# Graph attention on one Trainium2 core: the dots of a chunk as one product and one sum

## The chip, the cores and the metric

The kernel runs on one core of a Trainium2 chip (trn2). The metric is the device time of one execution in microseconds, as the median of several executions.

## The reference

One graph attention layer over 12500 nodes with 64 features and 212500 edges sorted by target node, followed by a residual sum and a layer norm:

```python
h_trans = features @ Watt_w.T + Watt_b
h_src, h_dst = h_trans[src], h_trans[dst]
e_raw = jnp.sum(h_dst * jnp.tanh(h_src + e_r), axis=-1, keepdims=True)
e_ij = leaky_relu(e_raw / out_dim ** 0.5)
exp_e = jnp.exp(e_ij - segment_max(e_ij, dst)[dst])
alpha = exp_e / (segment_sum(exp_e, dst)[dst] + 1e-09)
h_neigh = segment_sum(features[src] * alpha, dst)
h_out = leaky_relu((features + h_neigh) @ W1_w.T + W1_b + (features * h_neigh) @ W2_w.T + W2_b)
x = layernorm(x + h_out)
```

The change is in `e_raw`: for each edge, the product of two vectors of 64 values and its sum.

## The kernel before

The edges are cut into 111 blocks of 1920. A block is 15 tiles of 128 edges: partition p holds 15 consecutive edges of the list, so every tile is a column of 64 values a partition. The 15 tiles form four chunks (4, 4, 4 and 3 tiles); chunks 0 and 1 are piece 0, chunks 2 and 3 piece 1. The last block has 11 tiles in chunks of 4, 4, 2 and 1. The edges of a block hit at most 128 consecutive nodes, its window.

Every engine has its own written order of work, one `step` a block, and a step works on several blocks at once: `b`, the one before it (`prev`), the two before that (`before`, `third`) and the next ones (`nxt`, `ahead`, `far`). The steps of four blocks are the body of a loop on the four engines that compute; the first and last blocks stand outside it. What a block goes through:

- GpSimd (POOL) gathers the source rows of its 15 tiles from a table in HBM, one indirect DMA a tile (`gather`, L628), into one of four buffers `got`. The gathers of a piece wait until VectorE has read that piece of the block four before (`scale_rows`, L1290, wait at L626). ScalarE builds `hotT`, the one-hot matrices of the targets (`offsets` L724, `mark_nodes` L735).
- TensorE (PE) expands the window's rows `hw` to one row an edge (`expand`, L949): 15 fp32 products, two passes each, into four PSUM banks `ps_hd[c]`, one a chunk. It starts on a block once `lay_back` (L975) of the block before is issued, which waits for VectorE's `scan_row` (L1257, L1259).
- VectorE adds the gathered row to the edge's attributes (`add`, L1221), ScalarE takes the tanh in place (`tanh`, L750), and VectorE makes the dots (`dot`, L1232): one multiply-and-sum instruction a tile, with the product written back to `edge` and the sum to one column of `raw`. In the trace each is a CUSTOM_DVE_ANT_0 and a DVE_READ_ACCUMULATOR2_ANT.
- `finish_scores` (L1244 to L1250) and `scan_row` find the largest score of each target. In the next step `exponents` (L1266 to L1276), ScalarE's `probabilities`, `scale_rows`, and the split of the scaled rows into three bf16 parts (`left_part` L1297, `low_part` L1303 on VectorE, `high_part` L785 and `mid_part` L790 on ScalarE) feed the sums on TensorE (`sum_edges`, L994). Then come the dense layer and the norm.

VectorE's order in a step is: add of chunk 0, exponents of `prev`, `place(nxt)` (two copies, L1196 and L1198, then `dst_rel`, L1199, which waits on a semaphore for the second copy), the four `build_hot` (L1210), both `scale_rows`, the node work of two older blocks, `set_gaps`, dot 0, add 1, both `left_part`, dot 1, add 2, both `low_part` (the second waits for ScalarE's second `mid_part`), add 3, dot 2, dot 3, `finish_scores`, `scan_row`, and the norm of `third`. Nothing else sets the order.

Of the kernel before, what the change touches and what calls it, by code (L numbers as in the profile page):

```python
# [22 lines left out]
ALU = mybir.AluOpType  # L23
ACT = mybir.ActivationFunctionType
AX = mybir.AxisListType
# [6 lines left out]
CHUNK = 4  # L32
# [21 lines left out]
def gnn_layer(nc, x, src, dst, edge_attr, w1, b1, w2, b2, watt, batt, out):  # L54
    N, D = x.shape
# [29 lines left out]
    SCALE = D ** -0.5  # L85
# [7 lines left out]
    with ExitStack() as ctx:  # L93
        def sb(name, shape, dt=F32):
            return ctx.enter_context(nc.sbuf_tensor(name, shape, dt))

        def bank(name, dt=F32):
            return ctx.enter_context(nc.psum_tensor(name, [P, 512 * 4 // mybir.dt.size(dt)], dt))

        def sem(name):  # L100
            return ctx.enter_context(nc.semaphore(name))

        def by_chunk(name):

            return [sem(f"{name}_{c}") for c in range(NC)]
# [52 lines left out]
        edge = [sb(f"edge{k}", [P, TILES, D]) for k in range(2)]  # L158
        got = [sb(f"got{k}", [P, TILES, 2 * D + 1]) for k in range(BUFS)]

        hw = [sb(f"hw{k}", [P, D]) for k in range(2)]
# [3 lines left out]
        hotT = [sb(f"hotT{k}", [P, TILES, P]) for k in range(2)]  # L165
        raw = [sb(f"raw{k}", [P, TILES]) for k in range(2)]
# [74 lines left out]
        ps_hd = [bank(f"ps_hd{k}") for k in range(CHUNK)]  # L241
# [66 lines left out]
        hd_ready = by_chunk("hd_ready")  # L308
        added = by_chunk("added")
        tanh_done = by_chunk("tanh_done")  # L310
        scored = by_chunk("scored")
        here_set = sem("here_set")
        ids_set = sem("ids_set")
# [78 lines left out]
        def chunks(b):  # L392
            return FINAL_CHUNKS if final(b) else CHUNKS
# [8 lines left out]
        def follows(b, n):  # L402

            return not b.known or b.n >= n

        def cols(b, c):
            return chunks(b)[c][0], chunks(b)[c][-1] + 1
# [5 lines left out]

            return 16 * (b.fours * len(CHUNKS[c]) + len(chunks(b)[c]))

        def expanded(g, c):

            k = g % CHUNK
            return ps_hd[c][:, k * D:(k + 1) * D]

        def node_rows(t, b, a, z):
# [453 lines left out]
        def _(pe):  # L875
# [64 lines left out]
            def expand(b, c):  # L940

                pe.wait_ge(hotT_built[c // 2], b.n + 1)
                if c == 0:
                    pe.wait_ge(h_in[b.two], (b.twos + 1) * 16)
                if follows(b, 1):

                    pe.wait_ge(scored[c], b.n)
                for g in range(*cols(b, c)):
                    last = pe.matmul(expanded(g, c), hotT[b.two][:, g, :], hw[b.two][:, :], start=True, stop=True)  # L949
                last.then_inc(hd_ready[c], 1)  # L950

            def lay_rows(b):
# [65 lines left out]
            def step(third, before, prev, b, nxt, ahead, far):  # L1018
                if exists(third):
                    dense(third)  # L1020
                if exists(b):
                    for c in range(NC):
                        expand(b, c)
                if exists(before):
                    transpose_sum_prod(before)
                if exists(prev) and carried(prev):
                    take_carry(before)
                if exists(prev):
                    sum_edges(prev, 0)
                    sum_edges(prev, 1)  # L1030
                if exists(b):
                    lay_rows(b)
                    lay_back(before, b)
# [39 lines left out]
        def _(dve):  # L1073
# [150 lines left out]
            def dot(b, c):  # L1224

                a, z = cols(b, c)

                dve.wait_ge(consts, 5)
                dve.wait_ge(tanh_done[c], b.n + 1)
                dve.wait_ge(hd_ready[c], b.n + 1)  # L1230
                for g in range(a, z):
                    last = dve.tensor_tensor_reduce(  # L1232
                        out=edge[b.two][:, g, :], in0=edge[b.two][:, g, :],
                        in1=expanded(g, c), scale=SCALE, scalar=0.0,
                        op0=ALU.mult, op1=ALU.add, accum_out=raw[b.two][:, g:g + 1])
                last.then_inc(scored[c], 1)

            def gap_of(b):
                return gap_final if final(b) else gap
# [133 lines left out]
            def step(third, before, prev, b, nxt, ahead, far):  # L1373
# [18 lines left out]
                if exists(b):  # L1392
                    set_gaps(b)
                    dot(b, 0)
                    add(b, 1)
# [3 lines left out]
                if exists(b):  # L1399
                    dot(b, 1)  # L1400
                    add(b, 2)
# [4 lines left out]
                if exists(b):  # L1406
                    add(b, 3)
                    dot(b, 2)
                    dot(b, 3)
                    finish_scores(b)  # L1410
                    scan_row(b)
# [127 lines left out]
```

## Time and profile before

| | |
|---|---|
| median of 3 executions | 2827.87 us (2823.59 to 2828.71) |
| the profiled execution | 2813.21 us |
| its span | 2811.4 us |
| instructions | 32328 |
| PE, share of the span | 49% |
| VectorE (DVE) | 59% |
| ScalarE (ACT) | 57% |
| GpSimd (POOL) | 59% |
| DMA | 296.07 MB, mean 105 GB/s |

The span is the time from the first to the last instruction of one profiled execution. The granted clock of TensorE is 0.5 of full speed in all but the first of 40 slices of the span. The busy shares hardly vary over the span. No engine is busy for more than three fifths of it, so the busy time by itself does not say what the kernel waits for; the timeline of one block does. A line of the timeline gives start and length in microseconds, the engine, the line of the code, the operation, what it writes and reads, how many instructions are merged in it, and in square brackets the idle time before it with what ended it.

### The profile page before, as it was taken

Reading aid. Unit: us, or ns where it says so; the run is one execution under the profiler, and the core shown is the slowest. Engines: PE = TensorE matmul, PEld = TensorE weight load, DVE = VectorE, ACT = ScalarE, POOL = GpSimd, SP = SyncE. Lnnn points to the kernel's source line nnn. Section 1 sums busy time; section 2 is a strip of 40 time slices with the busy share of each in tenths; the row PEclk is TensorE's granted clock in tenths of the full one; section 3 lists DMA queues with packets and bytes.
Section 4 is the critical chain, followed back from the end, with each engine's and each line's share of the span. In section 5 each row is a group of like instructions: output and inputs, shape, how many; then the busy total and the mean of one; then the engine's idle time right before and its main releaser. Section 6 shows DMA issues by size and latency. Waiting matters only on the chain. (4 is left out here: it accounts for less than half of the span.)

```text
span 2811.4 us, 32328 instructions
## 1 busy us (share of the span) xinstructions
PE 1365.9 (49%) x6440; PEld 1096.9 (39%) x6440; DVE 1652.8 (59%) x7936; ACT 1602.6 (57%) x2794; POOL 1655.3 (59%) x1670
## 2 busy tenths in 40 slices
PE   4344444455444444554445444554544555444455
PEld 4333343344333433443334334443433444333344
DVE  2256666655665656565666555655666556566567
ACT  2345555565555555565655556655555565656565
POOL 4466666666665666566666656666566666666660
PEclk7555555555555555555555555555555555555555
DMA  4333333333333333333333333333333333333331
GB/s 162 113 94 101 108 109 108 108 107 97 109 101 107 108 108 108 108 95 105 105 108 109 108 108 100 116 100 100 104 108 109 108 102 102 110 100 108 108 111 31
DMA packets 169270, 296.07 MB, mean 105 GB/s; under 512 B 111730, under 2 KB 111942, under 8 KB 169107
## 3 DMA queue, kind: packets, MB, share of 16 engines
q1 hardware_dynamic: 114689, 185.75, 19.9%
q0 software_dynamic: 53152, 107.98, 15.5%
q14 instruction: 154, 1.26, 0.1%
q10 hardware_dynamic: 1266, 0.93, 0.1%
q8 instruction: 9, 0.15, 0.0%
HBM read 284.43 MB, written 10.07 MB: 105 GB/s over the span
## 5 line engine op out<-in xcount | busy, mean ns | idle before, releaser
L628 POOL DMA_INDIRECT got<-table,src_i x1631 | 1625.7, 997 | 1074.5 <-DVE spare L1290 515.4
L949 PE MATMUL ps_hd<-hw,hotT 128*128 128x64 f32 x3322 | 731.9, 421 | 7.3 <-ACT hotT L735 7.3
L949 PEld LDWEIGHTS ps_hd<-hw,hotT 128*128 128x128 f32 x3322 | 721.9, 333 | 7.5 <-ACT hotT L735 7.5
L994 PE MATMUL ps_acc<-parts,hot 128*128 128x195 bf16 x1661 | 328.3, 364 | 637.9 <-DVE parts L1303 567.2
L750 ACT ACTIVATE edge<-edge 128x256 f32<-128x256 f32 (+1 forms) x444 | 176.6, 398 | 613.8 <-issue 499.8
L994 PEld LDWEIGHTS ps_acc<-parts,hot 128*128 128x128 bf16 x1661 | 208.8, 136 | 744.9 <-issue 619.8
L724 ACT ACTIVATE off<-dst_all,node 128x1024 bf16<-128x1024 int32 x222 | 424.7, 1913 | 121.3 <-remote 73.6
L1303 DVE TENSOR_TENSOR parts<-spare,parts 128x520 bf16<-128x520 f32 x222 | 147.1, 663 | 235.1 <-ACT parts L790 211.8
L1232 DVE CUSTOM_DVE_ANT_0 edge<-edge,ps_hd 128x64 f32<-128x64 f32 x1661 | 265.8, 217 | 18.8 <-remote 7.1
L1005 PE MATMUL ps_misc<-ident,sum_prod 128*128 128x128 f32 x111 | 52.4, 472 | 431.7 <-DVE sum_prod L1319 431.7
L735 ACT ACTIVATE hotT<-off,ones 128x1024 f32<-128x1024 bf16 x222 | 242.6, 1093 | 7.2
L1199 DVE TENSOR_SCALAR dst_rel<-dst_i,base 128x30 bf16<-128x30 int32 (+1 forms) x111 | 27.1, 244 | 365.3 <-remote 262.5
L1221 DVE TENSOR_TENSOR edge<-edge,got 128x256 f32<-128x256 f32 (+1 forms) x444 | 178.8, 403 | 76.3 <-issue 76.3
L1005 PEld LDWEIGHTS ps_misc<-ident,sum_prod 128*128 128x128 f32 x111 | 20.9, 188 | 451.5 <-DVE sum_prod L1319 451.5
L1210 DVE TENSOR_TENSOR hot<-ps_row,dst_rel 128x512 bf16<-128x512 bf16 (+1 forms) x444 | 149.8, 400 | 41.3 <-DVE dst_rel L1199 29.7
L785 ACT ACTIVATE parts<-spare 128x520 bf16<-128x520 f32 x222 | 133.4, 604 | 66.8 <-DVE spare L1290 64.5
L774 ACT ACTIVATE prob<-arg 128x15 f32<-128x15 f32 (+1 forms) x111 | 23.9, 215 | 252.2 <-remote 145.8
L1257 DVE TENSOR_TENSOR_SCAN ps_row<-row_gap,row_max,ps_row 1x256 f32<-1x256 f32 x109 | 81.0, 743 | 134.3 <-remote 52.7
L790 ACT ACTIVATE parts<-spare 128x520 bf16<-128x520 f32 x222 | 134.9, 608 | 24.2 <-DVE spare L1297 20.2
L975 PE MATMUL ps_misc<-ident,row_max 1*128 1x1 f32 x222 | 40.6, 250 | 217.7 <-issue 193.8
L798 ACT ACT_TABLE_LOAD x109 | 139.8, 1283 | 2.0
L975 PEld LDWEIGHTS ps_misc<-ident,row_max 1*128 1x128 f32 x222 | 34.5, 202 | 270.0 <-issue 270.0
(137 smaller groups left out, 1974.1 us busy)
## 6 DMA issues: line engine op xcount, KB each, us to landing
dst_all<-in_dst SPq DMA_DIRECT2D x109, 960.5 KB
edge<-in_edge_attr SPq DMA_DIRECT2D x110, 480.0 KB
got<-table,src_i POOLq DMA_INDIRECT x1631
table<-hx SPq DMA_DIRECT2D x12, 512.0 KB
hw<-table SPq DMA_DIRECT2D x111, 32.0 KB
xw<-in_x SPq DMA_DIRECT2D x111, 32.0 KB
out<-y_out SPq DMA_DIRECT2D x111, 32.0 KB
x_piece<-in_x SPq DMA_DIRECT2D x3, 768.0 KB, 4.4
```

The lines of the kernel that those rows point to most:

```text
L628: pool.indirect_dma_start(got[b.four][:, g, 0:2 * D], None, table, bass.IndirectOffsetOnAxis(ap=src_i[b.four][:, g:g + 1], axis=0))\
L724: act.activation(off[p][:, 0:z - a, :], ids[:, a:z, :], ACT.Abs, bias=node[b.two][:, 0:1])\
L735: act.activation(hotT[b.two][:, a:z, :], off[p][:, 0:z - a, :], ACT.Relu, bias=ones[:, 0:1], scale=-1.0)\
L750: act.activation(edge[b.two][:, a:z, :], edge[b.two][:, a:z, :], ACT.Tanh).then_inc(tanh_done[c], 1)
L790: act.activation(parts[:, a:z, 1, :], rest[:, a:z, :], ACT.Copy).then_inc(rest_mid[p], 1)
L798: act.activation(std1[:, :], mean_var[:, 1:2], ACT.Sqrt, bias=eps_col[:, 0:1]).then_inc(std_set, 1)
L949: last = pe.matmul(expanded(g, c), hotT[b.two][:, g, :], hw[b.two][:, :], start=True, stop=True)
L994: last = pe.matmul(a_parts, hot[b.four][:, g, :], parts[:, g, :, :].rearrange("p a d -> p (a d)"), start=(g == 0), stop=(g == tiles(b) - 1))
L1210: dve.tensor_tensor(hot[b.four][:, a:z, :].rearrange("p g (n a) -> p g n a", a=2), row_iota.rearrange("p (z n a) -> p z n a", z=1, a=2).to ...
L1221: dve.tensor_tensor(edge[b.two][:, a:z, :], edge[b.two][:, a:z, :], got[b.four][:, a:z, 0:D], ALU.add).then_inc(added[c], 1)
L1232: last = dve.tensor_tensor_reduce(out=edge[b.two][:, g, :], in0=edge[b.two][:, g, :], in1=expanded(g, c), scale=SCALE, scalar=0.0, op0=ALU ...
L1303: dve.tensor_tensor(parts[:, a:z, 2, :], rest[:, a:z, :], parts[:, a:z, 1, :], ALU.subtract)\
```

## The change

The dots of a chunk become two instructions. The first multiplies all tiles of the chunk by the expanded rows of the chunk's PSUM bank and by the scale, in place in `edge`. The second sums `edge` along its 64 columns and writes the chunk's columns of `raw`. VectorE waits for the first through a new semaphore a chunk, `multiplied`, before it issues the second. A tile's place in the bank now counts from the first tile of its chunk, which is the same place as before but in the last block's last chunk.

```diff
--- before.py
+++ after.py
@@ -308,6 +308,7 @@
         hd_ready = by_chunk("hd_ready")
         added = by_chunk("added")
         tanh_done = by_chunk("tanh_done")
+        multiplied = by_chunk("multiplied")
         scored = by_chunk("scored")
         here_set = sem("here_set")
         ids_set = sem("ids_set")
@@ -413,9 +414,9 @@
 
             return 16 * (b.fours * len(CHUNKS[c]) + len(chunks(b)[c]))
 
-        def expanded(g, c):
-
-            k = g % CHUNK
+        def expanded(g, b, c):
+
+            k = g - cols(b, c)[0]
             return ps_hd[c][:, k * D:(k + 1) * D]
 
         def node_rows(t, b, a, z):
@@ -946,7 +947,7 @@
 
                     pe.wait_ge(scored[c], b.n)
                 for g in range(*cols(b, c)):
-                    last = pe.matmul(expanded(g, c), hotT[b.two][:, g, :], hw[b.two][:, :], start=True, stop=True)
+                    last = pe.matmul(expanded(g, b, c), hotT[b.two][:, g, :], hw[b.two][:, :], start=True, stop=True)
                 last.then_inc(hd_ready[c], 1)
 
             def lay_rows(b):
@@ -1228,12 +1229,12 @@
                 dve.wait_ge(consts, 5)
                 dve.wait_ge(tanh_done[c], b.n + 1)
                 dve.wait_ge(hd_ready[c], b.n + 1)
-                for g in range(a, z):
-                    last = dve.tensor_tensor_reduce(
-                        out=edge[b.two][:, g, :], in0=edge[b.two][:, g, :],
-                        in1=expanded(g, c), scale=SCALE, scalar=0.0,
-                        op0=ALU.mult, op1=ALU.add, accum_out=raw[b.two][:, g:g + 1])
-                last.then_inc(scored[c], 1)
+                dve.scalar_tensor_tensor(
+                    out=edge[b.two][:, a:z, :], in0=edge[b.two][:, a:z, :], scalar=SCALE,
+                    in1=ps_hd[c][:, 0:(z - a) * D].rearrange("p (g d) -> p g d", d=D),
+                    op0=ALU.mult, op1=ALU.mult).then_inc(multiplied[c], 1)
+                dve.wait_ge(multiplied[c], b.n + 1)
+                dve.tensor_reduce(raw[b.two][:, a:z], edge[b.two][:, a:z, :], AX.X, ALU.add).then_inc(scored[c], 1)
 
             def gap_of(b):
                 return gap_final if final(b) else gap
```

## Rows read from the trace of the kernel before

**Rows 1.** Part 1 of the page, busy time of each engine and its share.

```profile
PE 1365.9 (49%) x6440; PEld 1096.9 (39%) x6440; DVE 1652.8 (59%) x7936; ACT 1602.6 (57%) x2794; POOL 1655.3 (59%) x1670
```

**Rows 2.** Groups by line: op, count, busy us, mean ns, idle before by releaser.

```profile
L628 POOL DMA_INDIRECT got<-table,src_i x1631 | 1625.7, 997 | 1074.5 <-DVE spare L1290 515.4 <-issue 464.7 <-DMA src_i<-in_src 64.9
L1199 DVE TENSOR_SCALAR dst_rel<-dst_i,base 128x30 bf16<-128x30 int32 (+1 forms) x111 | 27.1, 244 | 365.3 <-remote 262.5 <-issue 99.1 <-DVE base L1198 3.2
```

**Rows 3.** Timeline, ordinary block: start us, length us, engine, line, idle before.

```profile
1404.44 6.61 PE L949 MATMUL ps_hd<-hw,hotT 128*128 128x64 f32 x30
1406.15 0.15 DVE L1198 COPY base<-base_all 128x1 f32 x1
1408.04 0.95 POOL L628 DMA_INDIRECT got<-table,src_i  x1 [0.30 <-issue]
1410.50 0.24 DVE L1199 TENSOR_SCALAR dst_rel<-dst_i,base 128x30 bf16<-128x30 int32 x1 [4.19 <-issue]
1411.20 1.35 DVE L1210 TENSOR_TENSOR hot<-ps_row,dst_rel 128x512 bf16<-128x512 bf16 x4 [0.46 <-DVE dst_rel L1199]
1413.96 0.94 POOL L628 DMA_INDIRECT got<-table,src_i  x1 [4.97 <-DVE spare L1290]
```

**Rows 4.** Timeline of a block in which the gathers had ended before the expansion.

```profile
1285.88 6.61 PE L949 MATMUL ps_hd<-hw,hotT 128*128 128x64 f32 x30
1289.72 0.24 DVE L1199 TENSOR_SCALAR dst_rel<-dst_i,base 128x30 bf16<-128x30 int32 x1
1292.84 0.94 POOL L628 DMA_INDIRECT got<-table,src_i  x1 [8.47 <-DVE spare L1290]
```

**Rows 5.** Timeline, two blocks whose expansion started later against the gathers.

```profile
1889.39 6.61 PE L949 MATMUL ps_hd<-hw,hotT 128*128 128x64 f32 x30
1898.64 0.95 POOL L628 DMA_INDIRECT got<-table,src_i  x1 [5.23 <-DVE spare L1290]
...
1674.64 6.61 PE L949 MATMUL ps_hd<-hw,hotT 128*128 128x64 f32 x30
1683.70 0.95 POOL L628 DMA_INDIRECT got<-table,src_i  x1 [5.53 <-DVE spare L1290]
```

**Rows 6.** Timeline of VectorE, the dots of the ordinary block and their neighbours.

```profile
1416.83 0.22 DVE L1232 CUSTOM_DVE_ANT_0 edge<-edge,ps_hd 128x64 f32<-128x64 f32 x1
1417.40 0.42 DVE L1221 TENSOR_TENSOR edge<-edge,got 128x256 f32<-128x256 f32 x1
1417.74 1.24 DVE L1297 TENSOR_TENSOR spare<-spare,parts 128x520 f32<-128x520 f32 x2
...
1422.64 0.64 DVE L1303 TENSOR_TENSOR parts<-spare,parts 128x455 bf16<-128x455 f32 x1 [2.15 <-ACT parts L790]
1424.06 0.22 DVE L1232 CUSTOM_DVE_ANT_0 edge<-edge,ps_hd 128x64 f32<-128x64 f32 x1
1424.61 0.17 DVE L1244 SCALAR_TENSOR_TENSOR score<-raw 128x15 f32<-128x15 f32 x1
```

**Rows 7.** Groups by line and form: durations that cost the new instructions.

```profile
L1232 DVE CUSTOM_DVE_ANT_0 edge<-edge,ps_hd 128x64 f32<-128x64 f32 x1661 | 265.8, 217 | 18.8 <-remote 7.1 <-issue 5.0 <-ACT edge L750 2.8
L1221 DVE TENSOR_TENSOR edge<-edge,got 128x256 f32<-128x256 f32 x332 | 139.6, 421 | 75.5 <-issue 75.5
L1324 DVE SCALAR_TENSOR_TENSOR z<-z 128x64 f32<-128x64 f32 x111 | 25.5, 229 | 0.1
L1340 DVE TENSOR_TENSOR y_new<-xw,z 128x64 f32<-128x64 f32 x111 | 25.0, 225 | 3.8
L1310 DVE TENSOR_REDUCE sums<-ps_acc 128x65 f32<-128x195 f32 x111 | 39.1, 352 | 0.0
L1109 DVE TENSOR_REDUCE falls<-hotT 125x1 f32<-125x1699 f32 x1 | 1.9, 1922 | 0.0
```

**Rows 8.** Timeline of a block with a short wait of the gathers.

```profile
1362.28 1.35 DVE L1210 TENSOR_TENSOR hot<-ps_row,dst_rel 128x512 bf16<-128x512 bf16 x4 [0.47 <-DVE dst_rel L1199]
1365.27 0.95 POOL L628 DMA_INDIRECT got<-table,src_i  x1 [4.47 <-DMA src_i<-in_src]
```

## The prediction, made before the change was run

> **What bounds the kernel now.** I read the busy shares first: three engines stand at 57 to 59% [rows 1], so none is full, and a sum of busy times gives no time. The groups by line say who waits. GpSimd's gathers take 0.997 us each and have 0.30 us between them inside a block; 15 of them are 15 x 0.997 + 14 x 0.30 = 19.2 us. Before the first of a block GpSimd waits, nearly always for VectorE's `scale_rows` (515.4 us in all), now and then for the list of sources (64.9 us) [rows 2]. On VectorE the one large wait is before `dst_rel`: 365.3 us, 3.3 us a block [rows 2]. In the code that instruction waits only for the copy before it.
>
> The timeline of an ordinary block shows how the two hang together [rows 3]. The copy ends at 1406.30, yet `dst_rel` starts at 1410.50. Meanwhile the last gather ends at 1408.99 (1413.96 less 4.97), and TensorE expands from 1404.44 to 1411.05. After `dst_rel` come the one-hot matrices at 1411.20 and `scale_rows`, and with that GpSimd starts on its next 15 gathers, 4.97 us after its last one. In a block in which the gathers had ended (1284.37, from 1292.84 less 8.47) before TensorE began at 1285.88, `dst_rel` started 3.84 us after that beginning with no wait; in the ordinary block it was 6.06 us [rows 3, 4]. So an increment of a semaphore reaches its waiter late while gathers and fp32 expansion overlap. I can't say from this trace why, but what ends it is the end of the gathers. From the start of the matrices to the next gather it is always 2.76 us (1411.20 to 1413.96). In the second block of [rows 5] the gathers ended at 1678.17 and started again at 1683.70, so the matrices started at 1680.94, before the expansion was over at 1681.25; in the ordinary block they start 2.21 us after the last gather, here 2.77.
>
> That closes a loop: gathers 19.2 us, about 5.0 us until VectorE has got past `dst_rel` and `scale_rows`, gathers again, 24.2 us a block. VectorE's and ScalarE's own path from `scale_rows` to the next expansion is shorter and ends in the stall. The dots lie on that path, behind `scale_rows` and ahead of the expansion of the next block.
>
> **The dots themselves.** Today a chunk of four takes 0.57 us from its first instruction to the start of the add behind it, and the last chunk 0.55 us until the score starts [rows 6]. That is 0.14 us a tile: the recorded 0.217 us overlap [rows 7].
>
> The product is one instruction over 256 columns. At 64 columns this kind takes 0.229 us where a plain two-operand instruction takes 0.225, and the plain one takes 0.421 at 256 [rows 7], so 0.425 us. One input in PSUM I cost at nothing, since today's dots read it too. The wait on `multiplied`: an instruction that waits for the one before it starts 0.034 us after it (3.8 us over 111) [rows 7]; being a full wait it also takes away the overlap. Queued behind it are the sum, the next add, both `left_part` and so ScalarE's `mid_part`. The sum reads 256 columns; reductions take 0.352 us at 195 and 1.922 at 1699, 1.04 ns a column [rows 7], so 0.416 us, of which the next instruction sees 0.336 (0.42 long instructions follow each other at 0.34) [rows 6]. A chunk of four: 0.425 + 0.034 + 0.336 = 0.795, or +0.225. The last chunk, 192 columns: 0.36 + 0.034 + 0.349 + 0.034 = 0.777, or +0.23. A block: +0.9 us on VectorE, though 15 instruction pairs become 8 instructions. Below: the two passes over 256 columns are 0.53 us by themselves, so no gain comes from a pair unless it overlaps fully. Above: if the own wait meets a late increment such as the 0.46 us before the one-hot matrices [rows 3], each of the last two chunks costs that much more.
>
> A rule of the Trainium skill speaks the other way. Its page "VectorE: DVE Perf Modes", in the section on the TRN2 errata, charges a fixed 58 cycles an instruction (120 with a PSUM source) plus one a column at 0.96 GHz, and advises few large instructions. By it 15 tiles are an estimated 2.88 us and the four pairs 2.74, a gain of 0.13 us. The trace's 0.14 us a tile, against the 0.19 that the rule gives, is why I don't take it.
>
> **What of it is on the path.** Dot 0 stands ahead of add 1 and `left_part`, which start ScalarE's chain: +0.225. Dot 1 is covered: after it VectorE waits 2.15 us for ScalarE's second `mid_part` before the second `low_part` [rows 6], and 0.225 us comes out of that wait. If that cover were gone it would cost its 0.225. Dots 2 and 3 stand between that wait and `finish_scores`: +0.225 and +0.23. So the next expansion starts 0.68 us later against `scale_rows`. SyncE's loads behind the store of the norm are issued later by the same; the buffers that they fill are wanted a block later, at no cost but for the list of sources.
>
> **What comes of it.** The gathers of a block still start right after `scale_rows`, ahead of the dots, and end when they did. The expansion starts 0.68 us later, VectorE reaches `dst_rel` 3.84 us after that without a stall, at 1404.44 + 0.68 + 3.84 = 1408.96, still 1.5 us before the 1410.50 of today. So the lengthening goes into the stall. Not all of it: the overlap of gathers and expansion is 4.55 us in the ordinary block, with a wait of GpSimd of 4.97; where it is 4.02 the wait is 5.23, and where it is 3.53 the wait is 5.53 [rows 3, 5]. An overlap of 4.55 - 0.68 = 3.87 gives 5.32 between these, +0.35. Some ordinary blocks have 5.2 already, so I take +0.3 us each for 95 blocks: 28.5 us. In about six blocks VectorE is late by itself, as in [rows 4], and with the three first and three last, where no gathers overlap, these twelve pay the full 0.68: 8 us. Sum 37 us. The profiled execution would go from 2813.2 to 2850; the median of the runs stands 14.7 us above it, and I add the 37 to the median: **2865 us**.
>
> **The rivals.**
> - *Fully exposed.* The stall is a fixed delay after the start of the expansion, not an end set by the gathers. Then every block pays 0.68, up to the full 0.9 if dot 1 isn't covered: 111 x 0.68 = 75 to 100 us, 2903 to 2928. For it: `dst_rel` comes at 6.06 us after the start in the ordinary block. Against: in [rows 4] it is 3.84.
> - *Fully absorbed.* GpSimd's wait stays at 4.97 and only the twelve blocks pay: 2836. For it: `dst_rel` would be ready 1.5 us before it starts today. Against: the rising waits of [rows 5].
> - *No longer on VectorE.* If the pair overlaps as today's tiles do, or a tile cost its full record, 15 x 0.217 = 3.26, which is also 3 x (0.425 + 0.416) + 0.36 + 0.349 = 3.23, nothing changes: 2828. The skill's rule above comes out here too. Against: the 0.57 us of a chunk [rows 6].
> - *Faster.* The place is the moment at which the late increments come free. It takes steps: in the block of [rows 8] the one-hot matrices start 1.48 us after the last gather (1360.80) and GpSimd waits 4.47 us, in the ordinary one 2.21 and 4.97. A later expansion has fewer increments queued when the gathers end. If the shift of 0.68 us puts most blocks on the earlier step, 95 x 0.5 us are won and 8 lost: 2788. It decides from where more than about one block in six goes there. Against: short waits appear only at the overlaps of 4.5 us and more, and [rows 5] go the other way.
>
> **How the numbers follow.** Partly absorbed, as forecast (its own range 2840 to 2890): 0.50. Fully exposed: 0.20. Fully absorbed: 0.12. No longer on VectorE: 0.07. Faster: 0.11. A measurement of this kernel can tell about 0.2% (5.7 us) from no change. The absorbed case lies 8 us up, close to that bound, and I split it in halves. Slower: 0.50 + 0.20 + 0.06 = 0.76. Same: 0.06 + 0.07 = 0.13. Faster: 0.11. The range leaves out the faster case and the upper end of the exposed one: 2826 to 2912.
>
> **What would show it.** Right: a product of about 0.43 us and a sum of about 0.41 in each chunk of four; the first dot to the add at 0.8 us; the wait before the second `low_part` down by some 0.2 us; the wait before `dst_rel` down from 3.3 us a block to about 2.9; GpSimd's wait before a block's first gather up from about 5.0 to 5.3 us with the gathers' 0.997 us unchanged. Wrong: a wait before `dst_rel` that stays at 3.3 us (exposed), a wait of GpSimd near 4.5 us (faster), late increments on `multiplied`, or gathers lengthened by the new instructions, which nothing in the trace lets me price.

## The result, and the profile after

The changed kernel takes 2887.5 us in the median (2871.4 to 2939.3, 4 runs), the kernel before beside it 2828.3 (2823.6 to 2829.3). The ratio is 1.0194, 95% interval 1.0149 to 1.0239: slower, by about 55 us (1.9%). Medians and ranges hold all executions; ratios leave out those over 1.5% above the fastest of their kernel, and four profiles below (the repeat of the change, the pair in the last two chunks, tiles with own waits, the spread pair) are of such ones, so that I read from them where time sits and not how much. The profiled execution took 2871.4 us against 2813.2.

The changed kernel's page (span and busy times, then the queue that fetches instructions: packets, MB, share of its engines), its groups by line, and the two dots by form:

```profile
span 2869.7 us, 29894 instructions
...
PE 1352.0 (47%) x6440; PEld 1091.2 (38%) x6440; DVE 1719.7 (60%) x5502; ACT 1593.0 (56%) x2794; POOL 1637.3 (57%) x1670
...
q14 instruction: 31, 0.25, 0.0%
...
L629 POOL DMA_INDIRECT got<-table,src_i x1631 | 1607.8, 986 | 1152.7 <-issue 612.3 <-DMA src_i<-in_src 454.4 <-DVE spare L1291 59.3
...
L1200 DVE TENSOR_SCALAR dst_rel<-dst_i,base 128x30 bf16<-128x30 int32 (+1 forms) x111 | 27.1, 244 | 4.1 <-issue 0.2
...
L1222 DVE TENSOR_TENSOR edge<-edge,got 128x256 f32<-128x256 f32 (+1 forms) x444 | 177.1, 399 | 7.4 <-issue 7.4
...
L1258 DVE TENSOR_TENSOR_SCAN ps_row<-row_gap,row_max,ps_row 1x256 f32<-1x256 f32 x109 | 81.0, 743 | 332.2 <-remote 259.2 <-PE ps_row L961 47.7 <-issue 25.3
...
L1232 DVE SCALAR_TENSOR_TENSOR edge<-edge,ps_hd 128x256 f32<-128x256 f32 x332 | 138.0, 416 | 169.2 <-ACT edge L751 75.7 <-remote 73.4 <-issue 11.9
...
L1237 DVE TENSOR_REDUCE raw<-edge 128x4 f32<-128x256 f32 x332 | 139.4, 420 | 13.7 <-DVE edge L1232 2.2 <-issue 0.3
```

The same for the kernel before, what [rows 1 to 8] don't hold:

```profile
q14 instruction: 154, 1.26, 0.1%
...
L1221 DVE TENSOR_TENSOR edge<-edge,got 128x256 f32<-128x256 f32 (+1 forms) x444 | 178.8, 403 | 76.3 <-issue 76.3
...
L1257 DVE TENSOR_TENSOR_SCAN ps_row<-row_gap,row_max,ps_row 1x256 f32<-1x256 f32 x109 | 81.0, 743 | 134.3 <-remote 52.7 <-PE ps_row L960 44.4 <-issue 37.2
```

GpSimd's line adds up to the result: against [rows 2] its gathers wait 1152.7 - 1074.5 = 78.2 us more and are busy 17.9 us less, 60.3 us for a span that is 58.3 longer. But what they wait for has changed. The stall ahead of `dst_rel`, 365.3 us before [rows 2], is 4.1 us. The wait ahead of the add has gone from 76.3 to 7.4 us, with the packets of code from 154 to 31. Ahead of the scan that reads `ps_row` 198 us have come, and 169.2 ahead of the product, where the tiles had 18.8 [rows 7]. VectorE is busy 67 us more than in [rows 1].

An ordinary block of the changed kernel in the timeline (start, length, engine, line, operation, idle before). The last gather of the block before it ends at 1410.26:

```profile
1406.47 0.15 DVE L1199 COPY base<-base_all 128x1 f32 x1
1406.66 0.24 DVE L1200 TENSOR_SCALAR dst_rel<-dst_i,base 128x30 bf16<-128x30 int32 x1
...
1412.57 0.15 DVE L1314 TENSOR_SCALAR den<-sums 128x1 f32<-128x1 f32 x1 [2.29 <-remote]
...
1415.11 0.42 DVE L1232 SCALAR_TENSOR_TENSOR edge<-edge,ps_hd 128x256 f32<-128x256 f32 x1
1415.57 0.42 DVE L1237 TENSOR_REDUCE raw<-edge 128x4 f32<-128x256 f32 x1
1415.90 0.42 DVE L1222 TENSOR_TENSOR edge<-edge,got 128x256 f32<-128x256 f32 x1
...
1421.15 0.64 DVE L1304 TENSOR_TENSOR parts<-spare,parts 128x455 bf16<-128x455 f32 x1 [1.94 <-ACT parts L791]
...
1421.96 0.42 DVE L1232 SCALAR_TENSOR_TENSOR edge<-edge,ps_hd 128x256 f32<-128x256 f32 x1
...
1423.52 0.17 DVE L1245 SCALAR_TENSOR_TENSOR score<-raw 128x15 f32<-128x15 f32 x1
```

`dst_rel` starts 0.04 us after the copy's end, though gathers run for another 3.6 us. From its norm's output at 1404.34 to the next at 1426.50 this block takes 22.2 us, less than before. What it costs comes in other blocks, all engines together:

```profile
1345.64 0.35 DVE L1222 TENSOR_TENSOR edge<-edge,got 128x192 f32<-128x192 f32 x1
...
1353.34 0.94 POOL L629 DMA_INDIRECT got<-table,src_i  x1 [0.30 <-issue]
1355.39 0.28 ACT L795 ACTIVATE sum_prodT<-ps_misc 128x128 f32<-128x128 f32 x1 [11.22 <-remote]
...
1357.39 0.42 DVE L1232 SCALAR_TENSOR_TENSOR edge<-edge,ps_hd 128x256 f32<-128x256 f32 x1 [11.40 <-ACT edge L751]
...
1369.08 1.17 POOL L629 DMA_INDIRECT got<-table,src_i  x1 [14.79 <-DMA src_i<-in_src]
```

After the add at 1345.64 neither VectorE nor ScalarE starts anything, while GpSimd gathers until 1354.29. 1.1 us after its last gather ScalarE gets on, and then VectorE. GpSimd's own next gather comes 14.79 us after its last, as the sources that SyncE loads are late with the rest. I call this a freeze. Worked out from the starts of `dst_rel` in the 111 blocks: before, the period is 24.5 us in the median and 24.1 in the mean, and 99 of 110 lie between 22 and 27. After, it is 22.9 and 24.6, from 18 to 38 but for two, and 29 lie between 22 and 27. The even rhythm has become one of short blocks and freezes.

Is it the increment that is late, or the engine that stands still behind it? The trace also records the updates of the semaphores, though not all of them. Of the 94 stalls of over 1 us ahead of `dst_rel` in the kernel before, 71 have the update for which it waits: it is recorded 1.0 to 5.7 us after the end of the copy (4.0 in the median) and 0.02 us ahead of the start of `dst_rel`. So there it is the increment that comes late. "remote" in the brackets marks this: an update on record with no instruction that ended near it. Behind the first 150 us the changed kernel has 118 such waits of over 1 us. Of the 31 over 8 us, 28 end with the last gather of a block or up to 4.7 us behind it. But 70 of the 118, nearly all short ones, end while gathers still run.

### The profile page after: what moved, and what is told of

It reads as the page before. It is cut to its first block and busy times, and to the rows that moved or that the text cites. A ratio compares the mean times of both kernels' runs of the same rounds, so it can differ in the third digit from the quotient of the medians.

```text
span 2869.7 us, 29894 instructions
## 1 busy us (share of the span) xinstructions
PE 1352.0 (47%) x6440; PEld 1091.2 (38%) x6440; DVE 1719.7 (60%) x5502; ACT 1593.0 (56%) x2794; POOL 1637.3 (57%) x1670
## 5 line engine op out<-in xcount | busy, mean ns | idle before, releaser
L629 POOL DMA_INDIRECT got<-table,src_i x1631 | 1607.8, 986 | 1152.7 <-issue 612.3
L1232 DVE SCALAR_TENSOR_TENSOR edge<-edge,ps_hd 128x256 f32<-128x256 f32 (+1 forms) x444 | 176.3, 397 | 169.2 <-ACT edge L751 75.7
L1237 DVE TENSOR_REDUCE raw<-edge 128x4 f32<-128x256 f32 (+1 forms) x444 | 178.7, 402 | 17.5 <-DVE edge L1232 2.2
L1291 DVE TENSOR_TENSOR spare<-got,prob 128x520 f32<-128x520 f32 x222 | 137.0, 657 | 0.6 <-ACT prob L775 0.6
L1298 DVE TENSOR_TENSOR spare<-spare,parts 128x520 f32<-128x520 f32 x222 | 137.3, 659 | 0.0
```

The source lines that it names most:

```text
L629: pool.indirect_dma_start(got[b.four][:, g, 0:2 * D], None, table, bass.IndirectOffsetOnAxis(ap=src_i[b.four][:, g:g + 1], axis=0))\
L1232: dve.scalar_tensor_tensor(out=edge[b.two][:, a:z, :], in0=edge[b.two][:, a:z, :], scalar=SCALE, in1=ps_hd[c][:, 0:(z - a) * D].rearrange( ...
L1237: dve.tensor_reduce(raw[b.two][:, a:z], edge[b.two][:, a:z, :], AX.X, ALU.add).then_inc(scored[c], 1)
```

## The experiments

"Even" below is the rhythm of before, "uneven" that of after; the two are told apart by the wait ahead of `dst_rel` and by what ended the waits of GpSimd. Not all were run on one chip, so each is compared by its ratio to the kernel before on the same chip, and times of different chips are not compared. The texts below speak of three theories: by the path theory the lengthened dots are the whole cost; by the code theory a larger loss is offset by fetches of code that are saved; the third, phase, is the forecast.

### The change again, and its code made long

The second kernel adds four satisfied waits behind each of four sorts of long instruction (one of the four places is shown):

```diff
                     ALU.is_equal).then_inc(hot_built[c], 1)
+                for _ in range(4):
+                    dve.wait_ge(consts, 5)
```

> The changed kernel once more, beside the three others of this call. Theory 1 (path): VectorE's lengthened dots are the whole cost. Theory 2 (code): the product and sum save 21 instructions a block on VectorE, the loop body no longer has to be fetched again each turn, and the measured time is the sum of a loss above 100 us and a gain of about 70. Both expect what was measured: a ratio of 1.015 to 1.024 to the kernel before, instruction-queue packets near 31 and almost no wait before dst_rel.

> The changed kernel with 20 more instructions a block on VectorE, all waits that are long satisfied, put behind long instructions: 1482 instructions in VectorE's program where the kernel before has 1504 and the changed one 1182. The work is the same. Theory 1 (path) expects no difference to the changed kernel, a ratio of 1.015 to 1.024. Theory 2 (code) expects the instruction queue back at about 150 packets, a wait of some 75 us in all before the add at the loop's turn, and 50 to 80 us more than the changed kernel, a ratio of 1.035 to 1.05. Theory 3 (phase) expects that with the fetches the old rhythm is back: a wait of about 300 us in all before dst_rel, and 2850 to 2870 us, a ratio of 1.008 to 1.015, which is the forecast made before the change was run.

Again: 1.0103 (0.9948 to 1.0258), median 2820.4 against 2783.2; uneven, 4.1 us ahead of `dst_rel`, 352.4 ahead of the product. On this chip both kernels vary more, and the interval holds 1: by itself this repeat doesn't show a loss. With long code: 1.0593 (1.0504 to 1.0681), 2931.1 us.

```profile
q14 instruction: 154, 1.26, 0.1%
...
L1224 DVE TENSOR_TENSOR edge<-edge,got 128x256 f32<-128x256 f32 (+1 forms) x444 | 178.7, 403 | 75.7 <-issue 75.6
...
L1200 DVE TENSOR_SCALAR dst_rel<-dst_i,base 128x30 bf16<-128x30 int32 (+1 forms) x111 | 27.1, 244 | 4.0
```

The packets are back at 154 and the wait ahead of the add is back at 75.7 us; the rhythm stays uneven. So the fetching belongs to the length of VectorE's program (1504 instructions before, 1482 here, 1182 in the change), and the change saves it: 68 us ahead of the add. This is the code theory, though its ratio of 1.035 to 1.05 was passed; the path theory, by which the waits cost nothing, and the return of the old rhythm are out. By the medians of all executions the kernel lost 110 us against the repeat, whose own four lie 94 us apart. So what is left besides the 68 is uncertain in size, and I can't divide it between the price of the waits themselves and what a late add sets off.

### Longer dots without the change

```diff
                 last.then_inc(scored[c], 1)
+                dve.tensor_tensor(idle[:, c, :], ident[:, :], ident[:, :], ALU.add)
```

First behind every chunk of the kernel before, then behind the last two with product and sum in the first two.

> The kernel before, its dots tile by tile, with one more instruction behind each chunk that adds 128 columns into a buffer that nobody reads: about 0.21 us more a chunk on VectorE, the length that the product and sum add, and 4 instructions a block more instead of 21 fewer. Theory 1 (path) expects the cost of the change: a ratio of 1.015 to 1.024. Theory 2 (code) expects the loss without the gain: 1.035 to 1.05. Theory 3 (phase, the forecast) expects the old rhythm with most of the lengthening taken out of the wait before dst_rel, which falls from 3.3 us a block to about 2.9: a ratio of 1.008 to 1.015.

> Product and sum in the first two chunks, as in the kernel that had this alone (even blocks of 24.3 us, a stall of 339.7 us ahead of dst_rel, 32 packets of code); the last two chunks stay tile by tile, each followed by an idle addition of 128 columns (0.286 us), so that the next expansion starts 0.57 us later, more than the 0.45 us that product and sum cost there. Is it the time of the expansion or the form of the last dots that lets the stall at dst_rel turn into long freezes? If the time: the stall under 50 us, blocks of 18 to 38 us, over 150 us idle ahead of the dots, a ratio of 1.01 to 1.03. If the form: the stall stays, 240 to 340 us, the period 24.3 us, a ratio of 1.00 to 1.015.

1.0129 (1.0013 to 1.0246), by the medians 2801.3 to 2783.2, 0.65%; and 1.0094 (1.0064 to 1.0125). The first kernel's groups, then the second's:

```profile
L1200 DVE TENSOR_SCALAR dst_rel<-dst_i,base 128x30 bf16<-128x30 int32 (+1 forms) x111 | 27.1, 244 | 269.4 <-remote 233.9 <-DVE base L1199 30.7 <-issue 4.5
...
L629 POOL DMA_INDIRECT got<-table,src_i x1631 | 1613.6, 989 | 1069.0 <-DVE spare L1292 569.6 <-issue 464.2 <-DMA table<-hx 26.3
...
1007.69 0.29 DVE L1238 TENSOR_TENSOR idle<-ident 128x128 f32<-128x128 f32 x1
1007.90 0.42 DVE L1222 TENSOR_TENSOR edge<-edge,got 128x256 f32<-128x256 f32 x1
```

```profile
L1201 DVE TENSOR_SCALAR dst_rel<-dst_i,base 128x30 bf16<-128x30 int32 (+1 forms) x111 | 27.1, 244 | 292.9 <-remote 262.6 <-issue 18.3 <-DVE base L1200 11.7
```

Both are even, at 24.3 us in the median. An idle addition is recorded with 0.286 us, but the next instruction starts 0.21 us behind its start, so it lengthens less than the second text takes. Measured in the median block from the first dot of a chunk to the add, or to the score, the first kernel is longer by 0.20 us in each of the first two chunks and by 0.24 in the last two together: 0.65 us a block, where the change has 0.22, 0.22 and 0.40, or 0.83. On the path, without the covered second chunk, it is 0.44 us, 49 us in all blocks, and for the second kernel 0.46 us. The first kernel's stall ahead of `dst_rel` is 96 us shorter than in [rows 2], and it lost 18 us by the medians. A loss well under the lengthening goes with the forecast and against the path theory, which leaves the stall alone; the intervals by themselves don't part the two. The code theory, which had 1.035 to 1.05, is out for this kernel. But GpSimd's wait, which by the forecast had to rise, did not: 1069.0 us against 1074.5 in [rows 2], though that trace is of another chip. So an expansion that comes up to 0.46 us later doesn't by itself make the rhythm uneven, whether the code is long or short; the change's full size was not tried with idle work.

### Product and sum in some chunks only

The first two chunks paired, the second alone, the last two; the others keep their tiles:

```diff
+                if c in (2, 3):      # (0, 2, 3) and (0, 1) in the other two
+                    for g in range(a, z):
+                        last = dve.tensor_tensor_reduce(
...
+                    last.then_inc(scored[c], 1)
+                    return
```

> Product and sum in chunks 0 and 1 alone, chunks 2 and 3 tile by tile: 1324 instructions in VectorE's program. Of the lengthening only chunk 0's 0.23 us is on the path, chunk 1's is covered by the wait before the second low_part. Theory 1 (path) expects a third of the cost, a ratio of 1.004 to 1.009. Theory 2 (code) expects it to depend on whether the fetches go: with them 1.005 to 1.015, without them (instruction queue near 31 packets) 0.98 to 1.0. Theory 3 (phase) expects the old rhythm if the fetches stay and 1.00 to 1.005.

> One part of the change alone: product and sum in the second chunk, tile by tile in the other three. Its dots end under the wait for ScalarE's second mid_part, which the prediction gives as cover: at no cost on the path. The path theory: no difference to the kernel before, within 0.2%. The code theory: VectorE's program is 1414 instructions long, between 1504 (154 packets of code in the trace, 76 us ahead of the add) and 1324 (32 packets, 7 us). If the packets are gone here too, 40 to 76 us ahead of the add go, which is at most 2.7% faster; how much of it comes through depends on the stall ahead of dst_rel, which would take it up (366 to 430 us there) and leave the time equal. If the packets stay at 154, nothing changes.

> Product and sum in the third and fourth chunk alone, the half of the change that stands right ahead of the scores and the next expansion: 0.45 us later a block; the first two chunks tile by tile. With the first two chunks alone the blocks stayed even at 24.3 us, the stall at 340 us and the ratio at 1.013; with all four the stall is 4 us and freezes of 10 to 15 us come in. If the later expansion alone turns the one into the other, this kernel shows it: the stall ahead of dst_rel under 50 us and idle time of over 150 us ahead of the product in the third chunk. If the lengthening has to pass some sum (0.68 us), it stays as before: a stall of 300 to 360 us, a period of 24.3 us, and a ratio of 1.00 to 1.01.

First two: 1.0128 (1.0040 to 1.0216). Second alone: 1.0099 (1.0075 to 1.0123). Last two: 2856.7 us in the median (2804.5 to 2863.5) against 2814.2 (2811.4 to 2815.8), without an interval. In that order:

```profile
L1200 DVE TENSOR_SCALAR dst_rel<-dst_i,base 128x30 bf16<-128x30 int32 (+1 forms) x111 | 27.1, 244 | 339.7 <-remote 268.6 <-issue 69.9 <-DVE base L1199 0.3
```

```profile
L1200 DVE TENSOR_SCALAR dst_rel<-dst_i,base 128x30 bf16<-128x30 int32 (+1 forms) x111 | 27.1, 244 | 316.7 <-remote 305.0 <-issue 8.5 <-DVE base L1199 2.9
...
L629 POOL DMA_INDIRECT got<-table,src_i x1631 | 1621.2, 994 | 1099.1 <-DVE spare L1299 524.7 <-issue 464.5 <-DMA src_i<-in_src 76.9
```

```profile
L1200 DVE TENSOR_SCALAR dst_rel<-dst_i,base 128x30 bf16<-128x30 int32 (+1 forms) x111 | 27.1, 244 | 4.0
...
L629 POOL DMA_INDIRECT got<-table,src_i x1631 | 1613.6, 989 | 1125.1 <-issue 642.4 <-DMA src_i<-in_src 406.4 <-DVE spare L1299 48.0
```

All three have 32 or 33 packets of code, so a program of 1414 instructions is short enough and one of 1482 is not. Only the pair in the last two chunks makes the rhythm uneven: 4.0 us ahead of `dst_rel`, and GpSimd waits for `src_i` (406.4 us) instead of for VectorE (48.0). The first two are even by the stall, though 10 of their 110 periods are over 27 us, where the kernel before has 5; by the code theory they had to gain. In the last two the one profile is of an execution at 2858.6 us, while the fastest of the four, at 2804.5, is under all of the kernel before, so this kernel shows the rhythm and no sure loss. Both theories missed the second chunk alone. Its dots are covered and its code is short, yet it is 1% slower; in the even rhythm the saved 69 us ahead of the add bring nothing, and why it loses is not settled (GpSimd waits 5.26 us a block in the median where before it is 5.18, which is 9 us of 24).

### Without the gathers

The same edit in the kernel before and in the changed one (the counts that are waited for, and the constants in place of the sources, go with it and are not shown):

```diff
-                    for g in chunks(b)[c]:
+                    for g in chunks(b)[c][0:1]:
                         pool.indirect_dma_start(got[b.four][:, g, 0:2 * D], None, table,
```

> The kernel before, with only the first of a chunk's gathers (4 of a block's 15); the sources of the other 11 tiles are constants, so 11 of 15 gathers are left out. It is the base for the same edit of the changed kernel. If late increments belong to the overlap of gathers with the expansion, the stall ahead of dst_rel (3.3 us a block with all gathers) goes to under 0.5, the loop through GpSimd is gone, and VectorE with ScalarE set the period: 24.2 less the stall and less the 1.5 us that they were early, some 19 to 21 us a block, 2250 to 2450 us. If the late increments come from something else (the fp32 products alone), the stall stays near 3 us and the time above 2600.

> The changed kernel with the same 11 of 15 gathers left out. Against the kernel before with few gathers: the path theory says plus 0.68 to 0.9 us in 111 blocks, 75 to 100 us slower, nothing given back. The code theory says that this is offset by the wait ahead of the add, 2.8 us in each of 27 turns of the loop, 76 us: between 0 and 25 us slower. The theory that the changed kernel freezes only where gathers run says that no wait of over 5 us is left ahead of the product, and that the blocks' periods are even; if freezes belong to the pair itself, they stay: over 100 us idle ahead of the product.

2211.5 us (2210.6 to 2212.6), under the 2250 expected, and 2206.0 (2203.2 to 2206.2), which is less than any of the theories had. Tiles first (the dst_rel row is duration of least, median, most in ns, then first and last start in us), then its timeline; the pair after it:

```profile
L1199 DVE TENSOR_SCALAR dst_rel<-dst_i,base x111: 234/244/246, 88.5 to 2163.3; 128x30 bf16<-128x30 int32 x110, 128x22 bf16<-128x22 int32 x1
...
L1221 DVE TENSOR_TENSOR edge<-edge,got 128x256 f32<-128x256 f32 (+1 forms) x444 | 178.6, 402 | 69.0 <-issue 69.0
...
DVE parts L1303 <- ACT parts L790: 235.4, 109, 2.2
...
1014.79 0.21 DVE L1232 CUSTOM_DVE_ANT_0 edge<-edge,ps_hd 128x64 f32<-128x64 f32 x1
...
1015.94 0.17 DVE L1244 SCALAR_TENSOR_TENSOR score<-raw 128x15 f32<-128x15 f32 x1
```

```profile
L1200 DVE TENSOR_SCALAR dst_rel<-dst_i,base x111: 235/244/246, 85.5 to 2152.9; 128x30 bf16<-128x30 int32 x110, 128x22 bf16<-128x22 int32 x1
...
L1222 DVE TENSOR_TENSOR edge<-edge,got 128x256 f32<-128x256 f32 (+1 forms) x444 | 177.1, 399 | 7.3 <-issue 7.3
...
DVE parts L1304 <- ACT parts L791: 211.8, 109, 2.0
...
1008.05 0.41 DVE L1232 SCALAR_TENSOR_TENSOR edge<-edge,ps_hd 128x256 f32<-128x256 f32 x1
...
1009.60 0.17 DVE L1245 SCALAR_TENSOR_TENSOR score<-raw 128x15 f32<-128x15 f32 x1
```

With few gathers there is no stall at `dst_rel` (3.9 and 4.1 us in all), no freeze, and the blocks are alike but for the turns of the loop; behind the first 50 us neither trace has a "remote" wait of over 1 us. Leaving gathers out takes away both GpSimd's work and the transfers that it starts, so these runs don't say which of the two makes increments late. The last two chunks take 1.15 us by tiles and 1.55 by pairs, +0.40; the first chunk costs +0.23; the second comes out of the wait for `mid_part`, 235.4 down to 211.8. On the path that is 0.63 us by these durations, where I had 0.68. But the 110 periods from the first `dst_rel` to the last sum to 2074.8 us by tiles and 2067.4 by pairs: the add waits 61.7 us less. Leave that out, and pairs cost 54.3 us, 0.49 a block, less than the durations say. So in the path alone the change is a small gain, 0.25%, and freezes come only with the gathers.

### What makes the rhythm uneven

The new wait alone, in the kernel before, then the whole change with its sums moved away from their products (`dot` keeps the product, `total` holds the wait and the sum):

```diff
                     op0=ALU.mult, op1=ALU.add, accum_out=raw[b.two][:, g:g + 1])
+                    if g == z - 2:
+                        last.then_inc(multiplied[c], 1)
+                        dve.wait_ge(multiplied[c], b.n + 1)
```

```diff
                     dot(b, 2)
                     dot(b, 3)
+                    total(b, 2)
+                    total(b, 3)
```

> The kernel before, tile by tile; the last tile of each chunk waits for an increment of a semaphore by the tile ahead of it. This is the new wait of the change (one increment and one wait a chunk, four a block) without its product and sum. It costs the overlap with the tile ahead, some 0.08 to 0.2 us a chunk. If the four increments more are what brings the long freezes, the stall ahead of dst_rel goes under 50 us and the periods spread from 18 to 38 us. If not, the blocks stay at 24.3 to 24.5 us with a stall of 270 to 365 us, and the ratio is 1.00 to 1.01.

> The whole change with its sums moved: sum 0 stands behind add 1, sum 1 behind add 2, sums 2 and 3 behind both their products, so that another long instruction stands between each product and the wait for it. Instructions, increments and waits are as many as in the change. If it is VectorE's wait for the instruction right before it, in the last two chunks above all, that lets the stall ahead of dst_rel turn into freezes of 10 to 15 us (the kernel before with nothing but such waits was 2.6% slower), this kernel keeps the even rhythm: a stall of 200 to 340 us ahead of dst_rel, periods of 24.3 us, under 50 us idle ahead of the product, and a ratio of 0.995 to 1.012. If any increment and wait more does it, or the short program, it goes as the change does: a stall under 50 us, periods of 18 to 38 us, over 150 us idle ahead of the product or late in the block, a ratio of 1.01 to 1.03. From the first dot of a chunk to the add it is shorter either way, since product and add follow each other at 0.34 us.

```profile
L1200 DVE TENSOR_SCALAR dst_rel<-dst_i,base 128x30 bf16<-128x30 int32 (+1 forms) x111 | 27.1, 244 | 88.9 <-remote 54.0 <-issue 28.3 <-DVE base L1199 3.9
...
L1233 DVE CUSTOM_DVE_ANT_0 edge<-edge,ps_hd 128x64 f32<-128x64 f32 x1661 | 296.3, 218 | 251.6 <-remote 112.9 <-ACT edge L751 61.6 <-issue 53.1
...
1038.58 0.22 DVE L1233 CUSTOM_DVE_ANT_0 edge<-edge,ps_hd 128x64 f32<-128x64 f32 x1
...
1039.27 0.42 DVE L1222 TENSOR_TENSOR edge<-edge,got 128x256 f32<-128x256 f32 x1
```

```profile
L1200 DVE TENSOR_SCALAR dst_rel<-dst_i,base 128x30 bf16<-128x30 int32 (+1 forms) x111 | 27.1, 244 | 4.1 <-issue 0.2
...
L1232 DVE SCALAR_TENSOR_TENSOR edge<-edge,ps_hd 128x256 f32<-128x256 f32 x332 | 138.6, 417 | 446.0 <-ACT edge L751 272.9 <-remote 113.3 <-issue 36.3
```

One increment and one wait a chunk, with no product and no sum, make the kernel 1.0259 times as long (1.0192 to 1.0326): as much as the whole change, or more. They lengthen a chunk by 0.12 us only (0.69 from first tile to add, against 0.57 [rows 6]). The stall at `dst_rel` falls from 365.3 to 88.9 us and 251.6 us appear ahead of the tiles. I had put its ratio at up to 1.01 if this was not the cause, and the mark for "is the cause", a stall under 50 us, wasn't reached; but its periods run from 18 to 40 us but for two, with 45 of 110 under 22 as in the changed kernel, and that is the other mark. All this is read from an execution at 2908.8 us; its own three fastest are at 2844 to 2859. On the last two chunks its waits lie 0.20 us longer than the tiles, less than the 0.24 of the idle additions, which left the rhythm even. The spread pair is at 1.0229 (1.0154 to 1.0304) and fully uneven. Its waits mostly find the increment there (the sums sat idle for 5.3 us in all). So my finer theory, that VectorE has to stand at the wait, has fallen.

### The expansion taken away

In the changed kernel:

```diff
-                for g in range(*cols(b, c)):
+                for g in range(*cols(b, c))[0:None if b.known and b.n == 0 else 1]:
                     last = pe.matmul(expanded(g, b, c), hotT[b.two][:, g, :], hw[b.two][:, :], start=True, stop=True)
```

> The changed kernel with all its gathers, but behind the first block only one of a chunk's expansion products in fp32: 11 of 15 are left out, and the dots read old values there. If late increments need both gathers and these products side by side, as the prediction had it, the freezes go: no wait of over 5 us ahead of the product, under 50 us idle there in all, and GpSimd's wait ahead of a block's first gather falls to 0.3 to 3 us, since the path of 18.9 us a block without gathers is under the 19.2 us of the gathers; 2250 to 2500 us. If gathers alone make increments late, the freezes stay: over 150 us idle ahead of the product, and above 2650 us.

2793.1 us (2763.0 to 2812.5) against 2779.3; ratio 1.0027 (0.9985 to 1.0069).

```profile
L1200 DVE TENSOR_SCALAR dst_rel<-dst_i,base 128x30 bf16<-128x30 int32 (+1 forms) x111 | 27.1, 244 | 4.1 <-issue 0.2
...
L1258 DVE TENSOR_TENSOR_SCAN ps_row<-row_gap,row_max,ps_row 1x256 f32<-1x256 f32 x109 | 81.0, 743 | 246.2 <-remote 179.5 <-PE ps_row L961 48.0 <-issue 18.7
...
DVE ps_row L1258 <- remote: 179.5, 31, 9.4
...
DVE raw L1237 <- remote: 81.6, 27, 4.7
```

The expansion is down from 731 to 217 us of TensorE, and waits of up to 9.4 us are still there, now ahead of the scan (ahead of the product it is 42.1 us in all, so only that mark was met). Here the sum's own wait for `multiplied` meets late increments too, 27 times and for up to 4.7 us, which in the change it doesn't. GpSimd's wait didn't fall as expected (1073.3 us in all), and the time isn't near 2500. So most of the expansion isn't needed for late increments, while the gathers, or what they start, are, as the runs with few of them showed. The prediction's "while gathers and fp32 expansion overlap" gave the second condition too much. That this kernel is about level with the one before, though uneven, I read as the price of the rhythm falling with a shorter expansion; no run tests that.

## Why the prediction was right, and where it was not

The time was right in sign and about in size: 2865 forecast, 2887.5 measured, inside the range and inside the forecast's own 2840 to 2890. The reasons were right in part, and that the sum came out is in part luck: its 37 us were 28.5 of a small even loss and 8 for twelve blocks, while the measured 59 are left over from larger terms of either sign, of which the forecast had only the dots.

- **The dots.** Product 0.416 us (0.425 forecast), sum 0.420 (0.416), first dot to add 0.79 (0.795), the last two chunks 1.56. These came from the nearest rows, and they held. The page of the Trainium skill that spoke the other way (VectorE: DVE Perf Modes, the TRN2 errata) gave an estimated gain of 0.13 us a block; the rows show a loss of about 0.82 us (0.22, 0.20, and 0.4 for the last two).
- **The cover of dot 1.** Right: the wait came down from 2.15 to 1.94 us, and without gathers from 2.24 to 2.02.
- **The path.** With few gathers 0.63 us by the durations and 0.49 by the periods, of 0.68 forecast.
- **The loop turn.** Missed, and the largest term that was to be had from the trace. The add's wait in [rows 7], 75.5 us ended by nothing that the profile shows, came in 27 pieces: three short ones at the start, then 24 of 2.9 to 3.5 us, some 98 us apart as the turns of the loop are, beside 154 packets of code. In the changed kernel these 24 are of 0.3 us. I wrote that 15 pairs of instructions become 8 and gave this no price. It was worth 62 to 69 us of VectorE's waits, as much as the dots cost.
- **"So the lengthening goes into the stall."** This is the step that failed for this change. For mere length the idle additions did show a shorter stall, though no rise of GpSimd's wait. With the change itself the stall ahead of `dst_rel` was to fall to 2.9 us a block and vanished, and GpSimd's wait rose by 0.7 us a block (78.2 over 108) through single waits of up to 17 us, while the median one fell from 5.2 to 4.8; it was to be an even 0.3. I took lateness for a property of the place, with a delay at `dst_rel` that a shift of 0.68 us can eat into. It is free to move: when `dst_rel` passes while gathers run, the lateness turns up elsewhere, as in the 11.22 us of ScalarE's copy of a TensorE result in the freeze and ahead of the scan of `ps_row`. Only the long ones end with the gathers.
- **The readings beneath.** The 2.76 us from the matrices to the next gather are not "always" so: they hold in 93 of the 107 waits of over 1 us ahead of a block's gathers, and in [rows 8] it is 2.99. And the wait of 4.97 us from which the 0.3 was counted is that of one block; the median is 5.2. At overlaps of 3.95 to 4.03 us the waits are 5.2 to 5.3, hardly above that, so the rise rested on two blocks and the base on a third.
- **The new wait.** I priced it at 0.034 us and the lost overlap. The kernel with nothing but these waits lost 2.6%. "Late increments on `multiplied`" stood among the things that would make me wrong, but not as a rival with a price. In the changed kernel itself the sum's idle time is 13.7 us in the chunks of four, so it isn't the wait's own length that costs.

Why more increments and waits in the last two chunks tip the rhythm is open. Six kernels that have them there were uneven (the change, with long code, spread, with few products, the last two chunks alone, tiles with own waits), and the five with all gathers that don't were even. What the runs rule out as needed: the short code (uneven with 154 packets too), the wait's standing time, product and sum as such, and a lengthening beyond that of the idle additions (0.20 us in the last two chunks by own waits is uneven, 0.24 by idle additions even). Whether the change's full 0.40 us there would be enough by itself was not tried. An increment's price while gathers run was not measured by itself, nor was the wait taken away, as the sum needs the product.

An account of the 58 us by which the profiled span grew is thus: VectorE's path longer by 0.63 x 111 = 70 (54 by the periods), the loop turn shorter by 69, and a remainder of 57 (73), which I put down to the uneven rhythm; it is what is left over, not a measurement, and it takes the path's lengthening at its full price, though in the even rhythm most of one was taken up. No kernel with all its work was faster than the kernel before.

## What to carry to other kernels

Add up the waits that come once for each turn of a loop and end in nothing that the profile shows, and look at the queue of instruction fetches: an edit that shortens the longest program can give back what its slower instructions cost. Where an even stall stands ahead of an instruction that has nothing to wait for, something else is holding increments, and a saving or a loss elsewhere doesn't simply flow into it. Count the semaphore increments and waits that an edit adds and where, not only their nanoseconds, and try them alone.

## What the runs showed of the hardware

- Fetches of VectorE's code: 154 packets with programs of 1482 and 1504 instructions, 31 to 33 with 1182 to 1414. With the long ones VectorE stood 2.9 to 3.5 us ahead of the first add of each turn of the loop (24 waits, 73.6 us, in the kernel before), with the short one of the change 0.3 us.
- Semaphore increments of VectorE and TensorE can stay out while GpSimd issues gathers back to back, and VectorE then waits up to 12.9 us in the changed kernel; no "remote" wait of over 1 us in any of the traces is for an increment of ScalarE. The long ones end with the last gather or up to 4.7 us behind it (28 of 31), the short ones mostly amid the gathers. With 4 gathers a block in place of 15 there was none behind the first 50 us; with 4 expansion products in place of 15 they were still there.
- Four increments and waits a block, 0.12 us for a chunk of four, went with 2.6% on the kernel.
- Two-operand additions of 128 columns are recorded with 0.286 us, and the next instruction starts 0.21 us behind their start; idle work of this kind costs the second number.
